# First layer's attention: the second half of each finished channel pair's split moved from step 25 to step 27 of its sixteen

## The chip, the core and the metric

The kernel runs on one core of one Trainium2 chip. The metric is the device time of one execution in microseconds; the figure shown for a kernel is the median of several executions. The profile is of one execution of its own.

The engines are called as the profile has them: PE is TensorE (matmul; PEld its weight load), DVE is VectorE, ACT is ScalarE, POOL is GpSimd, SP issues the DMAs.

## What is computed

Two layers over an input of 8 x 32 x 32 x 512, all in float32. Only the first is touched by the change. Cut to what matters, it is:

```python
x_norm = group_norm(x) * scale + bias                  # 32 groups of 16 channels
q, k, v = split(x_norm @ w_qkv + b_qkv)                # 8 heads of 64 channels, 1024 tokens, 8 images
weight = softmax((q * s) @ (k * s).T)                  # per image and head, 1024 x 1024
out = (weight @ v) @ w_out + b_out                     # (1)
x = x + out
```

The second layer is an attention with a depthwise convolution, sampled keys and values and an MLP. Products are made with operands in two parts, a rounded high part and the rest as a low part, so that three products of the parts stand for one in float32. "Split" below means making these two parts. For (1) the attention's result has to be split before it is multiplied with `w_out`.

## The kernel before

`layer0` goes through eight images. Per image there are the projections to q, k and v, then the attention over 8 heads, then the projection of the result with `w_out`, which runs together with the start of the next image. Each engine has its own program, written out by hand (`tensor_image`, `scalar_image`, `vector_image`, `gpsimd_image`, `sync_image`); semaphores tie them together. There is no scheduler: an engine does its instructions in the order of the code and waits where a count has not been reached.

**The attention's loop.** The 64 units of an image are 8 heads times 8 tiles of 128 query rows; the loop variable `i_` counts 64 steps and a few more at the end. In step `i_`, TensorE makes the scores of unit `i_` (lines L480 and L481, tile `a_ps`), transposes the exponentials of unit `i_`-2 (L495) and multiplies the transposed parts with v (L510). VectorE takes the row maximum of the scores (L647), ScalarE their exponential (L612, tile `a_prob`). The transposed tile is split: ScalarE writes the high part `ph` (L605, two per step) and VectorE the low part `pl` (L664, two per step). Two units make a block `b` of 256 queries of one head. On even steps ScalarE and VectorE add up the two halves of the block that was finished (L595 `a_fold_t`, L655 `a_fold_s`), VectorE takes reciprocals of row sums (L668), and GpSimd multiplies the block by them (L749), which writes the finished result over that head's q in the tile `qk`, all in SBUF.

**Staging.** A head needs its q and k in parts as well. SP copies them within SBUF (L397, L398, two heads ahead), and GpSimd makes the parts in the tiles `qs`, `kh` and `kl`: part 0 is a copy L725 and a two-input operation L727, part 1 the copies L731 and L734, part 2 the two-input operation L737. GpSimd takes a part before each of three consecutive blocks; for the heads staged while two heads of a pair run out, these stand between the L749 of the steps 24, 26, 28 and 30 (and again 16 steps later). L725 waits for the DMAs of the copies. L727 reads and writes SBUF only.

**The split in question.** Heads 2c and 2c+1 fill the 128 channels of pair `c`. When both are finished, `qk[:, c, :]` is split in two halves of 512 tokens: ScalarE copies to the high part `ah[c]` (L620) and VectorE subtracts it to the low part `al[c]` (L672), which reads two tiles of SBUF, `qk` and `ah`, and writes SBUF; the tiles show up as `a_a` in the profile. Both loops do this at the end of the steps in the table `SPLIT_AT`, which maps a step to a pair and a half. For the pairs 0 to 2 the steps are 23 and 25, 39 and 41, 55 and 57; the last pair goes in quarters after the loop. ScalarE waits for `att_ok`, the count of finished blocks (8 for pair 0), VectorE for ScalarE's part (`ah_ok`). The readers of the parts are the products with `w_out` in `out_tile`, which wait for six halves and come after step 64.

Of the kernel before, what the change touches and what calls it, by code (L numbers as in the profile page):

```python
# [24 lines left out]
CT = C // P  # L25
# [3 lines left out]
HALF = TOK // 2  # L29
# [53 lines left out]
def layer0(nc, x, gn_scale, gn_bias, w_qkv, b_qkv, w_out, b_out, x2, n_images=B):  # L83
# [7 lines left out]
    with ExitStack() as ctx:  # L91
# [90 lines left out]
        STAGE = 5  # L182
        AVERAGE_AT = 3
        POWER_AT = 3
        SPLIT_AT = {16 * c + 23 + 2 * s: (c, slice(s * HALF, (s + 1) * HALF)) for c in range(CT - 1) for s in range(2)}
        SPLIT_AT.update({U + 2 * j: (CT - 1, slice(256 * j, 256 * j + 256)) for j in range(NB)})
        SPLITS = 2 * (CT - 1)

# [188 lines left out]
        EACH.update({s.num: 16 * (U // 2 // ROWS) for s in iv_ld})  # L377
        EACH.update({staged.num: STAGE * NH, ah_ok.num: len(SPLIT_AT), al_ok.num: len(SPLIT_AT)})

# [184 lines left out]
        def scalar_image(act, r):  # L564
# [4 lines left out]
            def evict(g):  # L569

                kind, m, s = groups[g]
                act.wait_ge(pr_ps, at(pr_ps, g + 1))
                if r > 0 and g == 0:
                    act.wait_ge(al_ok, at(al_ok, 0))
                if r > 0 and g == 4:
                    act.wait_ge(o_st, at(o_st, 0))
                if kind == "v":
                    act.activation(v[:, :, m, 0:HD], by_head(ps[:, g % 8, :]), ACT.Copy).then_inc(vh_ok, 1)
                elif m < CT:
                    act.activation(qk[:, m, s * HALF:(s + 1) * HALF], ps[:, g % 8, :], ACT.Identity,  # L580
                                   bias=bq[:, m:m + 1], scale=QSCALE).then_inc(qk_sb, 1)
                else:
                    act.activation(qk[:, m, s * HALF:(s + 1) * HALF], ps[:, g % 8, :], ACT.Identity,
                                   bias=vec[:, 8 + m:9 + m]).then_inc(qk_sb, 1)
# [3 lines left out]
            for i_ in range(U + 7):  # L588
# [19 lines left out]
                if i_ < U:  # L608
# [6 lines left out]
                    if i_ < LATE:  # L615
                        evict(len(groups) - LATE + i_)
                if i_ in SPLIT_AT:
                    c, n = SPLIT_AT[i_]
                    act.wait_ge(att_ok, at(att_ok, 2 * NB * (c + 1) if c < CT - 1 else U // 2 - NB + (i_ - U) // 2 + 1))
# [9 lines left out]
        def vector_image(dve, r):  # L629
# [14 lines left out]
            for i_ in range(U + 7):  # L644
# [21 lines left out]
                if i_ >= 2 and i_ % 2 == 0 and i_ <= U:  # L666
                    dve.wait_ge(exp_ok, at(exp_ok, i_))
                    dve.reciprocal(row_inv[:, i_ - 2:i_], row_sum[:, i_ - 2:i_]).then_inc(inv_ok, 1)  # L668
                if i_ in SPLIT_AT:
                    c, n = SPLIT_AT[i_]  # L670
                    dve.wait_ge(ah_ok, at(ah_ok, list(SPLIT_AT).index(i_) + 1))
# [1275 lines left out]
def build(nc, a, out, n_images=B):  # L1947
    x2 = nc.dram_tensor("x2", [B, TOK, C], F32, kind="Internal").ap()
    l0 = [a["L0_conv_" + n] for n in ("gn_scale", "gn_bias", "w_qkv", "b_qkv", "w_out", "b_out")]
    layer0(nc, a["x"].rearrange("b h w c -> b (h w) c"), *l0, x2, n_images)  # L1950
    l1 = {n: a["L1_conv_" + n] for n in ("ln_g", "ln_b", "wq", "bq", "wv", "bv", "dw_w", "dw_b", "pw_w", "mq_w", "mq_b",
                                         "mk_w", "mk_b", "mv_w", "mv_b", "mo_w", "mo_b", "mlp_w", "mlp_b")}
    l1["dw_w"] = l1["dw_w"].rearrange("c o y x -> c (o y x)")
    l1["pw_w"] = l1["pw_w"].rearrange("k c y x -> k (c y x)")
    layer1(nc, x2, *l1.values(), out.rearrange("b h w c -> b (h w) c"), n_images)
# [17 lines left out]
```

## Time and profile before

| | us |
|---|---|
| median of 3 runs | 4020.2 |
| lowest, highest | 4017.14, 4028.37 |
| the profiled execution | 4022.35 |
| its span, first to last instruction | 4020.6 |

Mean granted TensorE clock over the span: 0.984. Of the span, the first 96.9 us go to the weights and the first image's start, and the eight attentions lie between 96.93 and 2272.32 us; the second layer takes about the last 1700. Between the attentions of two images there are some 98 us of projections.

A timeline row has the start, the duration, engine, line, operation and tiles as out<-in with their sizes; what stands in brackets is how long the engine sat idle before it and what ended that. Rows with x2 are two instructions in a row. Starts of neighbouring instructions on one engine can lie a little before the end of the one ahead. A windows row has the stretch, its length, the busy time of each engine, TensorE's granted clock as a share of 2.4 GHz, the DMA engines' share and GB/s.

### The profile page before, as it was taken

How to read it: one execution, taken by the hardware profiler on the slowest of the kernel's cores; microseconds unless marked ns; L12 is line 12 of the kernel's file. 1: busy time of each engine (PE TensorE's matmuls, PEld its weight loads, DVE VectorE, ACT ScalarE, POOL GpSimd, SP SyncE). 2: the span in 40 equal slices, each digit the busy share in tenths (PEclk: the TensorE clock that was granted, in tenths of full speed). 3: DMA queues.
4: the chain of work that ended last, by engine and by line, in shares of the span. 5: the costliest groups of instructions: out<-in, count | busy, mean ns of one | idle time of the engine just before them, and what ended most of it. 6: DMA issues, size and time to landing. Idle time of an engine off the chain costs nothing. (4 is left out here: it accounts for less than half of the span.)

```text
span 4020.6 us, 63404 instructions
## 1 busy us (share of the span) xinstructions
PE 3822.8 (95%) x21614; PEld 3202.9 (80%) x21614; DVE 2979.5 (74%) x5158; ACT 2433.8 (61%) x5241; POOL 1641.5 (41%) x1935
## 2 busy tenths in 40 slices
PE   8999999999999999999999889999999999999999
PEld 6888888888888888878888757777777777777777
DVE  3984984975966957939849747878787888787876
ACT  3873864755746837828738515656565656565656
POOL 1342432423432433324324305555545555555554
PEclk9999999999999999999999989999999999999999
DMA  2231331241241231322312222222222222222221
GB/s 87 53 75 44 65 75 43 53 89 41 54 90 36 54 80 41 62 67 54 77 47 59 74 96 69 74 74 74 74 74 74 75 75 73 75 73 75 73 74 59
DMA packets 175080, 269.32 MB, mean 67 GB/s; under 512 B 58732, under 2 KB 91560, under 8 KB 174760
## 3 DMA queue, kind: packets, MB, share of 16 engines
q1 hardware_dynamic: 170152, 248.48, 25.0%
q0 software_dynamic: 4608, 16.78, 1.4%
q8 instruction: 176, 2.88, 0.3%
q14 instruction: 144, 1.18, 0.2%
HBM read 113.90 MB, written 33.82 MB: 37 GB/s over the span
## 5 line engine op out<-in xcount | busy, mean ns | idle before, releaser
L647 DVE TENSOR_REDUCE a_neg_max<-a_ps 128x1 f32<-128x1024 f32 x512 | 622.3, 1217 | 313.9 <-PE a_ps L481 313.8
L605 ACT ACTIVATE a_ph<-a_ps 128x512 fp32r<-128x512 f32 x1024 | 565.8, 598 | 198.2 <-PE a_ps L495 196.8
L664 DVE TENSOR_TENSOR a_pl<-a_ps,a_ph 128x512 fp32r<-128x512 f32 x1024 | 655.4, 681 | 8.1 <-ACT a_ph L605 4.5
L749 POOL TENSOR_TENSOR a_qk<-a_fold_s,a_fold_r 64x256 f32<-64x256 f32 x256 | 192.5, 752 | 1060.9 <-DVE a_fold_s L655 840.5
L495 PE MATMUL a_ps<-a_ident,a_prob 128*128 128x128 f32 x4096 | 557.7, 278 | 56.7 <-DVE a_pl L664 55.6
L495 PEld LDWEIGHTS a_ps<-a_ident,a_prob 128*128 128x128 f32 x4096 | 464.3, 141 | 176.4 <-issue 113.6
L612 ACT ACTIVATE a_prob<-a_ps,a_neg_max 128x1024 f32<-128x1024 f32 x512 | 572.6, 1118 | 51.1 <-DVE a_neg_max L647 51.1
L510 PE MATMUL a_ps<-a_ph,a_v 128*128 128x256 f32 x2048 | 554.4, 303 | 0.0
L510 PE MATMUL a_ps<-a_pl,a_v 128*128 128x256 f32 x2048 | 513.2, 283 | 0.0
L481 PE MATMUL a_ps<-a_kl,a_qs 128*128 128x512 f32 x1024 | 406.4, 397 | 0.0
L480 PE MATMUL a_ps<-a_kh,a_qs 128*128 128x512 f32 x1024 | 404.7, 395 | 0.0
L1876 POOL TENSOR_SCALAR b_prob<-b_prob,b_row_inv 128x256 f32<-128x256 f32 x512 | 246.9, 482 | 366.7 <-DVE b_row_inv L1757 330.8
L510 PEld LDWEIGHTS a_ps<-a_pl,a_v 128*128 128x128 f32 x2048 | 392.5, 192 | 0.3
L510 PEld LDWEIGHTS a_ps<-a_ph,a_v 128*128 128x128 f32 x2048 | 389.0, 190 | 0.5 <-issue 0.2
L1651 DVE SCALAR_TENSOR_TENSOR b_ps<-b_qpad,b_dww,b_ps 128x256 f32<-128x256 f32 x704 | 294.2, 484 | 4.8
L1573 ACT ACTIVATE b_prob<-b_ps,b_neg_max 128x256 f32<-128x256 f32 x512 | 236.7, 483 | 42.8 <-DVE b_neg_max L1762 42.4
L1321 PE MATMUL b_ps<-b_qpad,b_diag 128*128 128x256 f32 x928 | 232.4, 409 | 0.0
L1321 PEld LDWEIGHTS b_ps<-b_qpad,b_diag 128*128 128x128 f32 x928 | 176.4, 190 | 50.9
L481 PEld LDWEIGHTS a_ps<-a_kl,a_qs 128*128 128x128 f32 x1024 | 195.2, 191 | 25.2
L725 POOL TENSOR_SCALAR a_kh<-a_qs 128x1024 fp32r<-128x1024 f32 x64 | 67.9, 1061 | 359.2 <-DMA a_kl<-a_qk 358.5
L480 PEld LDWEIGHTS a_ps<-a_kh,a_qs 128*128 128x128 f32 x1024 | 195.4, 191 | 22.2
L254 PE MATMUL a_ps<-a_xh,wqkv_hi 128*128 128x512 f32 x512 | 201.1, 393 | 5.6 <-DVE wqkv_lo L359 5.6
(262 smaller groups left out, 9218.7 us busy)
## 6 DMA issues: line engine op xcount, KB each, us to landing
a_qs<-a_qk SPq DMA_DIRECT2D x128, 256.0 KB, 4.3
a_kl<-a_qk SPq DMA_DIRECT2D x128, 256.0 KB, 4.8
a_xtok<-in_x SPq DMA_DIRECT2D x64, 256.0 KB, 5.4
a_fold_r<-a_inv_row SPq DMA_DIRECT2D x256, 64.0 KB, 3.6
b_xs<-x SPq DMA_DIRECT2D x64, 256.0 KB, 4.8
b_qs<-b_qh SPq DMA_DIRECT2D x64, 256.0 KB, 3.3
b_qs<-b_ql SPq DMA_DIRECT2D x64, 256.0 KB, 3.8
b_z<-x SPq DMA_DIRECT2D x64, 256.0 KB, 3.3
```

Source lines behind the costliest of these rows:

```text
L480: pe.matmul(bank, q_, kh[:, j, n], start=True, stop=False)
L481: mm = pe.matmul(bank, q_, kl[:, j, n], start=False, stop=True)
L495: mm = pe.transpose(ps[:, 4 + n % 2, kk * P:(kk + 1) * P], prob[:, u % 2, kt * P:(kt + 1) * P], ident[:])
L510: mm = pe.matmul(ps[:, 6 + b % 2, 0:256], v[:, h, kt, :], q_[:, b % 2, kt, :], start=kt == 0 and e == 0, stop=kt == TT - 1 and e == 1)
L605: act.activation(ph[:, b % 2, 4 * g:4 * g + 4, (u % 2) * P:(u % 2 + 1) * P], ps[:, 4 + n % 2, :].rearrange("p (k q) -> p k q", k=4), ACT.C ...
L612: act.activation(prob[:, i_ % 2, :], ps[:, 2 * (i_ % 2):2 * (i_ % 2) + 2, :] .rearrange("p a b -> p (a b)"), ACT.Exp, bias=neg_max[:, i_:i ...
L647: dve.tensor_reduce(neg_max[:, i_:i_ + 1], ps[:, 2 * (i_ % 2):2 * (i_ % 2) + 2, :] .rearrange("p a b -> p (a b)"), AX, ALU.max, negate=Tru ...
L664: dve.tensor_tensor(pl[here], ps[:, 4 + n % 2, :].rearrange("p (k q) -> p k q", k=4), raw(ph[here]), ALU.subtract).then_inc(pl_ok, 1)
L1321: mm = pe.matmul(ps[:, c, 0:NS], diag[:, e % DIAGS, :], window(c, n), start=first, stop=last)
L1573: act.activation(prob[:, u % 2, t, :], ps[:, 2 * (u % 2) + t // 2, (t % 2) * NK:(t % 2 + 1) * NK], ACT.Exp, bias=neg_max[:, c:c + 1], accu ...
L1651: dve.scalar_tensor_tensor(dst, window(c, n), dww[:, c, n:n + 1], grid(partial), ALU.mult, ALU.add).then_inc(tap, 1)
L1876: pool.tensor_scalar(prob[:, u % 2, t, :], prob[:, u % 2, t, :], row_inv[:, c:c + 1], 0.0, ALU.mult, ALU.add).then_inc(sc_ok, 1)
```

## The change

The second half of the pairs 0, 1 and 2 is split two steps later: at the steps 27, 43 and 59 instead of 25, 41 and 57. The first halves stay at 23, 39 and 55.

```diff
--- before.py
+++ after.py
@@ -182,7 +182,7 @@
         STAGE = 5
         AVERAGE_AT = 3
         POWER_AT = 3
-        SPLIT_AT = {16 * c + 23 + 2 * s: (c, slice(s * HALF, (s + 1) * HALF)) for c in range(CT - 1) for s in range(2)}
+        SPLIT_AT = {16 * c + 23 + 4 * s: (c, slice(s * HALF, (s + 1) * HALF)) for c in range(CT - 1) for s in range(2)}
         SPLIT_AT.update({U + 2 * j: (CT - 1, slice(256 * j, 256 * j + 256)) for j in range(NB)})
         SPLITS = 2 * (CT - 1)
```

On VectorE, steps 25 to 27 of the first image, before. `a_a_77` is the low part of pair 0, L647 begins a step:

```order
L647 TENSOR_REDUCE a_neg_max<-a_ps 128x1
L664 TENSOR_TENSOR a_pl<-a_ps,a_ph 128x4x128 x2
L672 TENSOR_TENSOR a_a_77<-a_qk,a_a_77 128x512
L647 TENSOR_REDUCE a_neg_max<-a_ps 128x1
L655 TENSOR_TENSOR a_fold_s<-a_ps,a_fold_t 64x256
L664 TENSOR_TENSOR a_pl<-a_ps,a_ph 128x4x128 x2
L668 RECIPROCAL a_row_inv<-a_row_sum 128x2
L647 TENSOR_REDUCE a_neg_max<-a_ps 128x1
L664 TENSOR_TENSOR a_pl<-a_ps,a_ph 128x4x128 x2
L647 TENSOR_REDUCE a_neg_max<-a_ps 128x1
```

and with the change:

```order
L647 TENSOR_REDUCE a_neg_max<-a_ps 128x1
L664 TENSOR_TENSOR a_pl<-a_ps,a_ph 128x4x128 x2
L647 TENSOR_REDUCE a_neg_max<-a_ps 128x1
L655 TENSOR_TENSOR a_fold_s<-a_ps,a_fold_t 64x256
L664 TENSOR_TENSOR a_pl<-a_ps,a_ph 128x4x128 x2
L668 RECIPROCAL a_row_inv<-a_row_sum 128x2
L647 TENSOR_REDUCE a_neg_max<-a_ps 128x1
L664 TENSOR_TENSOR a_pl<-a_ps,a_ph 128x4x128 x2
L672 TENSOR_TENSOR a_a_77<-a_qk,a_a_77 128x512
L647 TENSOR_REDUCE a_neg_max<-a_ps 128x1
```

L672 has moved behind the maximum L647, the fold L655, the splits L664 and the reciprocal L668 of two steps. It now stands between the last L664 of step 27 and the L647 of step 28.

On ScalarE, from the exponential of step 25 on, before (`a_a_77` is here the high part):

```order
L612 ACTIVATE a_prob,a_row_sum<-a_ps,a_neg_max 128x1024
L620 ACTIVATE a_a_77<-a_qk 128x512
L595 ACTIVATE a_fold_t<-a_ps 64x256
L605 ACTIVATE a_ph<-a_ps 128x4x128 x2
L612 ACTIVATE a_prob,a_row_sum<-a_ps,a_neg_max 128x1024
L605 ACTIVATE a_ph<-a_ps 128x4x128 x2
L612 ACTIVATE a_prob,a_row_sum<-a_ps,a_neg_max 128x1024
L595 ACTIVATE a_fold_t<-a_ps 64x256
```

and with the change:

```order
L612 ACTIVATE a_prob,a_row_sum<-a_ps,a_neg_max 128x1024
L595 ACTIVATE a_fold_t<-a_ps 64x256
L605 ACTIVATE a_ph<-a_ps 128x4x128 x2
L612 ACTIVATE a_prob,a_row_sum<-a_ps,a_neg_max 128x1024
L605 ACTIVATE a_ph<-a_ps 128x4x128 x2
L612 ACTIVATE a_prob,a_row_sum<-a_ps,a_neg_max 128x1024
L620 ACTIVATE a_a_77<-a_qk 128x512
L595 ACTIVATE a_fold_t<-a_ps 64x256
```

L620 has moved behind the exponentials of steps 26 and 27, and now stands right ahead of the fold copy L595 of step 28. The same happens for each pair and image. On TensorE, GpSimd and SP nothing stands in another place.

## Rows read from the trace of the kernel before

**Rows 1.** The page, section 1: busy us (share of the span), instructions
```profile
...
PE 3822.8 (95%) x21614; PEld 3202.9 (80%) x21614; DVE 2979.5 (74%) x5158; ACT 2433.8 (61%) x5241; POOL 1641.5 (41%) x1935
...
```

**Rows 2.** Windows of step 25 or 41 to 30 or 46: stretch and length, engines' busy us
```profile
...
734.07:751.83 17.76, 15.30 (x100) 13.87 (x99) 15.41 (x23) 12.58 (x24) 9.39 (x7) 0.90 0.10 21
...
1591.24:1606.44 15.20, 13.93 (x100) 12.38 (x99) 14.03 (x22) 12.51 (x24) 9.71 (x7) 1.00 0.21 44
...
1873.60:1888.08 14.48, 13.94 (x100) 12.39 (x99) 13.31 (x23) 12.52 (x24) 9.87 (x7) 1.00 0.21 47
...
2206.69:2223.04 16.35, 13.94 (x100) 12.39 (x99) 15.16 (x23) 12.53 (x24) 9.43 (x7) 1.00 0.10 22
sum 263.56, PE 233.47 PEld 208.29 DVE 235.18 ACT 200.51 POOL 152.64; mean PE 14.59 PEld 13.02 DVE 14.70 ACT 12.53 POOL 9.54
```

**Rows 3.** The same sixteen windows for line L672 alone: its busy time on VectorE
```profile
...
sum 263.56, DVE 32.41; mean DVE 2.03
```

**Rows 4.** Timeline of VectorE, third image, steps 25 to 28: start us, us, ...
```profile
...
737.07 2.60 DVE L672 TENSOR_TENSOR a_a<-a_qk,a_a 128x512 fp32r<-128x512 f32 x1 [0.61 <-ACT a_a L620]
739.60 1.21 DVE L647 TENSOR_REDUCE a_neg_max<-a_ps 128x1 f32<-128x1024 f32 x1
...
742.33 1.20 DVE L647 TENSOR_REDUCE a_neg_max<-a_ps 128x1 f32<-128x1024 f32 x1
...
746.32 1.23 DVE L647 TENSOR_REDUCE a_neg_max<-a_ps 128x1 f32<-128x1024 f32 x1 [1.14 <-PE a_ps L481]
```

**Rows 5.** Timeline of GpSimd, same image
```profile
...
736.74 2.38 POOL L727 TENSOR_TENSOR a_qs<-a_qs,a_kh 64x1024 fp32r<-64x1024 f32 x1
...
```

**Rows 6.** Timeline of TensorE, same image
```profile
...
741.88 1.94 PE L495 MATMUL a_ps<-a_ident,a_prob 128*128 128x128 f32 x8 [2.46 <-DVE a_pl L664]
...
```

**Rows 7.** Windows, same image: the column after POOL busy is TensorE's granted clock
```profile
...
743.00:745.00 2.00, 2.00 (x11) 2.00 (x10) 1.73 (x3) 1.74 (x3) 1.17 (x2) 0.50 0.21 37
...
```

**Rows 8.** Timeline of VectorE, seventh image, steps 23 to 29
```profile
...
1867.09 1.23 DVE L647 TENSOR_REDUCE a_neg_max<-a_ps 128x1 f32<-128x1024 f32 x1
...
1870.26 0.69 DVE L672 TENSOR_TENSOR a_a<-a_qk,a_a 128x512 fp32r<-128x512 f32 x1 [0.75 <-ACT a_a L620]
1870.87 1.22 DVE L647 TENSOR_REDUCE a_neg_max<-a_ps 128x1 f32<-128x1024 f32 x1
...
1873.60 1.20 DVE L647 TENSOR_REDUCE a_neg_max<-a_ps 128x1 f32<-128x1024 f32 x1
...
1876.60 0.69 DVE L672 TENSOR_TENSOR a_a<-a_qk,a_a 128x512 fp32r<-128x512 f32 x1 [0.61 <-ACT a_a L620]
1877.21 1.22 DVE L647 TENSOR_REDUCE a_neg_max<-a_ps 128x1 f32<-128x1024 f32 x1
...
1879.94 1.20 DVE L647 TENSOR_REDUCE a_neg_max<-a_ps 128x1 f32<-128x1024 f32 x1
...
1882.57 1.22 DVE L647 TENSOR_REDUCE a_neg_max<-a_ps 128x1 f32<-128x1024 f32 x1 [0.23 <-PE a_ps L481]
...
1885.33 1.23 DVE L647 TENSOR_REDUCE a_neg_max<-a_ps 128x1 f32<-128x1024 f32 x1
...
```

**Rows 9.** Timeline of GpSimd, seventh image
```profile
...
1878.29 2.37 POOL L727 TENSOR_TENSOR a_qs<-a_qs,a_kh 64x1024 fp32r<-64x1024 f32 x1
...
1882.69 1.05 POOL L734 TENSOR_SCALAR a_kh<-a_kl 128x1024 fp32r<-128x1024 f32 x1
...
```

**Rows 10.** Timelines of GpSimd and of VectorE, sixth image, step 25
```profile
...
1594.08 1.05 POOL L725 TENSOR_SCALAR a_kh<-a_qs 128x1024 fp32r<-128x1024 f32 x1 [3.16 <-DMA a_kl<-a_qk]
1595.21 2.69 POOL L727 TENSOR_TENSOR a_qs<-a_qs,a_kh 64x1024 fp32r<-64x1024 f32 x1
...
1594.24 1.42 DVE L672 TENSOR_TENSOR a_a<-a_qk,a_a 128x512 fp32r<-128x512 f32 x1 [0.61 <-ACT a_a L620]
...
```

**Rows 11.** Windows between the attentions of two images, columns as in rows 2
```profile
...
280.85:379.33 98.48, 95.11 (x461) 78.92 (x460) 37.74 (x64) 29.76 (x49) 30.03 (x22) 1.00 0.25 72
...
1702.15:1802.26 100.11, 96.73 (x461) 80.05 (x460) 37.28 (x64) 29.74 (x49) 30.28 (x23) 0.98 0.25 72
...
```

## The prediction

> **What bounds the kernel now.** I read four views in this order: the page's busy shares, the windows by stage, the timelines of single engines around steps 23 to 30, and the clock column of the windows.
>
> TensorE is 95% busy over the span [rows 1], but a mean over stages says nothing of this stretch. In the attention of layer one each step runs in a ring: TensorE makes scores, VectorE takes their maximum (L647), ScalarE the exponential (L612), TensorE transposes, ScalarE and VectorE split the transposed tile in two (L605, L664), TensorE uses it. A step is measured from one L647 to the next. Undisturbed it lasts 2.63 or 2.76 us [rows 8], so whatever stops VectorE for longer than the ring's slack stops TensorE too.
>
> The place to look at is the stretch from step 25 to step 30, which occurs 16 times with the next head's staging beside it (eight images, channel pairs 0 and 1). Its length should be the same each time, since its instructions are. It is not: the shortest is 14.48 us, others take 15.20, 16.35 or 17.76 us, and all sixteen take 263.56 us [rows 2]. Sixteen times 14.48 is 231.68, so **31.88 us** are lost there. Seven of the sixteen are like the 17.76, three like the 16.35, four are longer than 14.48 by up to 0.8, as the 15.20 is, and two stand at 14.48.
>
> The same windows for VectorE's split L672 alone show who loses it: 32.41 us for sixteen instructions [rows 3], where an undisturbed one takes 0.69 us [rows 8], that is 21.37 us too much. In the third image the split starts at 737.07 us and takes 2.60 [rows 4]; GpSimd's L727, a two-input operation of 2.38 us on SBUF, started at 736.74 and ends at 739.12 [rows 5]. The other nine long ones look alike: the split of step 25 lies on an L727 already running and waits for its end.
>
> The rest, 31.88 - 21.37 = 10.51 us, is TensorE's clock. After the held split TensorE stood idle for 2.46 us [rows 6], and just then its granted clock reads 0.50, which is 1.2 GHz instead of 2.4 [rows 7]; step 27 to 28 then lasts 746.32 - 742.33 = 3.99 us [rows 4] instead of 2.63 [rows 8]. Only the seven longest stretches show a clock below 1.00 (0.90 on average); 10.51 / 7 is 1.50 us each.
>
> **What the change does.** Per image and pair one ScalarE copy L620 and one VectorE split L672 move from the end of step 25 to the end of step 27. Nothing is added. The orders of TensorE, GpSimd and the SP queue, its DMAs among them, are the same; no queue is passed but VectorE's and ScalarE's own. Behind the moved pair on their engines stand the fold and the splits of step 28. Its wait for finished blocks (att_ok 8) was met before step 25 and stays met. Its output is wanted by the final projection only, steps later, so a later split costs no reader anything; even for pair 2, at step 59, the projection is several steps away.
>
> *Term one, the collision at step 25: -31.9 us.* With no split there, L727 meets only VectorE's L647, L655, L664 and L668: in the seventh image it ran beside them from 1878.29 to 1880.66, and step 26 still took 1879.94 - 1877.21 = 2.73 us [rows 8, 9]. All of the 21.37 us goes, and with it the TensorE pause and the 10.51 us at the low clock.
>
> *Term two, the split at step 27: does it meet GpSimd again?* What follows L727 there is the product L749 of a finished block, then two copies of the staging, L731 and L734, then a long idle until step 28's fold. In the undisturbed seventh image L727 starts at 1878.29 and L734 ends at 1882.69 + 1.05 = 1883.74, 5.45 us later [rows 9]. The split moves by how much? At step 25 it starts 1876.60 - 1873.60 = 3.00 us after L647; a split after an ordinary step, as step 23's is, starts 1870.26 - 1867.09 = 3.17 us after [rows 8]. Step 27 will be of that kind, and start 2.63 + 2.76 = 5.39 us after step 25's L647 (two steps of the kind that now follow, 1879.94 to 1882.57 to 1885.33 [rows 8]). So it moves by 5.39 + 3.17 - 3.00 = 5.56 us. In the ten long cases L727 starts about 0.33 us before the old split [rows 4, 5], so L734 ends 5.45 - 0.33 = 5.12 us after the old split's place, and the new split comes 0.44 us later than that. Clear, though not by much.
>
> In the late cases, where the DMA that releases L725 landed late, nothing is gained by the shift. In the sixth image L725 ends at 1594.08 + 1.05 = 1595.13, 0.89 us into the old split of 1594.24, which took 1.42 [rows 10], 0.73 more than 0.69: a split pays the overlap less 0.16. Afterwards L727 starts 0.08 behind, L734 ends at 1595.21 + 5.45 = 1600.66, and the new split wants to start at 1594.24 + 5.56 = 1599.80; overlap 0.86, price 0.70. So the four medium cases meet L734 for what they met L725 for. Their total is 21.37 less ten times 1.91 (2.60 - 0.69 [rows 4, 8]), 2.3 us. I add back **+2.3 us**. Pauses of that size were followed by no low clock (15.20 us at clock 1.00 [rows 2]).
>
> The Trainium skill bears on this term (SBUF — State Buffer, "Who interferes with whom"): a VectorE operation with two SBUF inputs and a GpSimd operation that reads SBUF exclude each other for a whole instruction, whichever shape they have. The trace agrees [rows 4, 5, 10], copies included. The rule speaks against the new place, for it makes L731 and L734 as able to block as L727; only their length is smaller. It gives no time by itself; the one it would give is that of the first rival below.
>
> *Term three, the ring's own cost of a split: +1.2 us.* Two splits two steps apart cost steps of 3.78, 2.73, 3.61, 2.73, 2.63, 2.76, 2.75 (step 23 to 30, 1867.09 to 1888.08: 20.99 us [rows 2, 8]). Four apart I expect 3.78, 2.73, 2.63, 2.76, 3.78, 2.73, 2.63 = 21.04, each number one of the same rows. That is +0.05, 24 times (pair 2 too). Bounds: 0, if the pair of steps costs the same, and +0.17 each (3.78 - 3.61), 4.1 us.
>
> **Sum**, against the profiled execution's 4022.35 us: 4022.35 - 31.9 + 2.3 + 1.2 = **3994 us**. The median of the three runs is 2 us lower; how often they collided isn't seen, and after the change the time depends little on that, so I keep 3994, 26 us (0.65%) under the median. A measurement can tell about 0.3% (12 us) from no change.
>
> **Rivals.**
> First, the copies take L727's place. The 0.44 us of clearance hangs on 5.39 us for two steps and on 3.17. Were the split a little over half a microsecond earlier, or GpSimd later, all would meet L734 [rows 9]. The price is at most its 1.05 less 0.16, 0.9 us, in the twelve places now free of it: +10.7, **4005 us**. For it: the thin margin. Against: in undisturbed stretches the steps repeat closely, as 2.73 us before and after the split of step 25 does [rows 8].
>
> Second, the slower clock appears elsewhere. Between two attentions a stretch takes 98.48 us, or 100.11 with clock 0.98 [rows 11], in two of seven cases; a later or earlier arrival of everything may make that none or seven: -3.3 to +8.1, **3991 to 4002 us**. The second layer has dips too, so some microseconds more may shift.
>
> Third, no gain: the collision only marks a place where the ring would wait anyway, for a later transfer or for scores. Then **4022 us**. Against: in the 14.48 us cases nothing waits [rows 2].
>
> Fourth, slower: L727 itself still runs when the new split comes. It must then start 5.56 + 0.33 - 2.38 = 3.5 us later than in the long cases (2.67 us into step 25, 3.00 - 0.33), so past 6.2 us into that step. The latest of the sixteen is the seventh image's, at 1878.29, 4.69 us into it [rows 8, 9]. The price is 1.91, with the low clock 3.41 us a place; in all sixteen 54.6, **4046 us**; with 30.7 us to be eaten up it turns the sign from ten places on. SP's order is unchanged, so nothing in the profile pushes it there.
>
> **How the numbers follow.** Forecast 0.78, first rival 0.11, second 0.05, third 0.04, fourth 0.02. The first two rivals are still faster than the bound of 4008. Faster by over 0.3%: 0.93, within: 0.05, slower: 0.02. The range: downwards the medium cases and the clock between attentions may vanish (2.3 + 3.3) and the second layer vary by a few, 3985; upwards the first rival and term three's upper bound, 4006.
>
> **What would show it.** Right: L672 long nowhere (no 2.6 us; a few between 0.7 and 1.5), the stretches from step 25 to 30 alike within 1 us, most at about 14.5 us, clock 1.00 in all of them, step 25 to 26 at 2.63 and step 27 to 28 at 3.78. First rival: L672 at 1 to 1.6 us in most of sixteen, behind L734. Wrong altogether: L672 at 2.6 us still, or L672 short and the stretches still 16 us or longer with another releaser in VectorE's idle time.

## The result, and the profile after

| | before | after |
|---|---|---|
| median, us | 4018.67 (4 runs) | 3994.9 (4 runs) |
| lowest, highest | 4016.38, 4028.37 | 3989.44, 4001.9 |
| the profiled execution | 4022.35 | 4001.9 |
| its span | 4020.6 | 4000.0 |

The ratio is 0.9936, 95% interval 0.9918 to 0.9954: faster by 0.64%. Ratios, here and below, are taken over all executions and differ a little from the quotient of the two medians. The forecast was 3994 us. A second measurement, beside other kernels, gave 0.9924 (0.9907 to 0.9940).

The page of the changed kernel, the line that answers to [rows 1]. TensorE's busy time is the same to 1 us, VectorE's is 21 us less:

```profile
...
PE 3823.4 (96%) x21614; PEld 3202.0 (80%) x21614; DVE 2958.2 (74%) x5158; ACT 2430.6 (61%) x5241; POOL 1640.5 (41%) x1935
...
```

The sixteen stretches of five steps from 25 or 41, answering to [rows 2], with columns as there:

```profile
...
211.79:226.99 15.20, 13.93 (x100) 12.38 (x99) 13.97 (x23) 12.56 (x24) 9.42 (x7) 1.00 0.21 40
447.65:462.19 14.54, 13.95 (x100) 12.39 (x99) 13.30 (x23) 12.57 (x24) 9.43 (x7) 1.00 0.10 21
...
1335.69:1350.81 15.12, 13.94 (x100) 12.39 (x99) 13.89 (x23) 12.57 (x24) 9.41 (x7) 1.00 0.18 40
...
sum 233.86, PE 223.07 PEld 198.22 DVE 214.12 ACT 201.04 POOL 150.97; mean PE 13.94 PEld 12.39 DVE 13.38 ACT 12.57 POOL 9.44
```

They came down from 263.56 to 233.86 us. Fourteen of them lie between 14.53 and 14.59 us, two at 15.12 and 15.20, and the clock is 1.00 in all. The same windows for L672 alone, answering to [rows 3] (it lies inside them, in step 27 or 43):

```profile
...
211.79:226.99 15.20, 1.36 (x1) 1.00 0.21 40
447.65:462.19 14.54, 0.69 (x1) 1.00 0.10 21
...
sum 233.86, DVE 12.39; mean DVE 0.77
```

12.39 us instead of 32.41. Sixteen undisturbed ones would be 11.09 (0.69 each), so of the 21.3 us for which the splits were held, 1.3 are left.

VectorE in the first image from step 25 on. L647 begins a step, and this answers to [rows 4, 8]:

```profile
...
165.45 1.20 DVE L647 TENSOR_REDUCE a_neg_max<-a_ps 128x1 f32<-128x1024 f32 x1
...
168.09 1.23 DVE L647 TENSOR_REDUCE a_neg_max<-a_ps 128x1 f32<-128x1024 f32 x1 [0.24 <-PE a_ps L481]
...
170.84 1.23 DVE L647 TENSOR_REDUCE a_neg_max<-a_ps 128x1 f32<-128x1024 f32 x1
...
174.01 0.69 DVE L672 TENSOR_TENSOR a_a<-a_qk,a_a 128x512 fp32r<-128x512 f32 x1 [0.75 <-ACT a_a L620]
174.62 1.22 DVE L647 TENSOR_REDUCE a_neg_max<-a_ps 128x1 f32<-128x1024 f32 x1
...
177.35 1.20 DVE L647 TENSOR_REDUCE a_neg_max<-a_ps 128x1 f32<-128x1024 f32 x1
...
179.99 1.23 DVE L647 TENSOR_REDUCE a_neg_max<-a_ps 128x1 f32<-128x1024 f32 x1 [0.24 <-PE a_ps L481]
```

Steps of 2.64, 2.75, 3.78, 2.73 and 2.64 us; the split starts 8.56 us after step 25 does. GpSimd beside it, answering to [rows 5, 9]:

```profile
...
168.17 2.39 POOL L727 TENSOR_TENSOR a_qs<-a_qs,a_kh 64x1024 fp32r<-64x1024 f32 x1
170.64 0.73 POOL L749 TENSOR_TENSOR a_qk<-a_fold_s,a_fold_r 64x256 f32<-64x256 f32 x1
171.46 1.05 POOL L731 TENSOR_SCALAR a_qs<-a_kh 64x1024 fp32r<-64x1024 f32 x1
172.60 1.05 POOL L734 TENSOR_SCALAR a_kh<-a_kl 128x1024 fp32r<-128x1024 f32 x1
176.30 0.73 POOL L749 TENSOR_TENSOR a_qk<-a_fold_s,a_fold_r 64x256 f32<-64x256 f32 x1 [2.65 <-DVE a_fold_s L655]
...
```

L734 ends at 172.60 + 1.05 = 173.65, the split comes at 174.01: 0.36 us apart. TensorE's longest pause in the steps 27 to 30 is now 0.59 us, where 2.46 stood [rows 6]:

```profile
...
176.91 1.17 PE L495 MATMUL a_ps<-a_ident,a_prob 128*128 128x128 f32 x8 [0.59 <-DVE a_pl L664]
...
```

The eight attentions, from the first L647 of an image to its last, before and then after, in the sum line of the windows by stage:

```profile
...
sum 1482.83, PE 1430.66 PEld 1263.17 DVE 1343.03 ACT 1220.80 POOL 555.54; mean PE 178.83 PEld 157.90 DVE 167.88 ACT 152.60 POOL 69.44
```

```profile
...
sum 1453.67, PE 1420.43 PEld 1253.18 DVE 1321.68 ACT 1219.45 POOL 553.39; mean PE 177.55 PEld 156.65 DVE 165.21 ACT 152.43 POOL 69.17
```

They gave 29.2 us. The whole span fell by only 20.6 in these two executions, because the second layer, which the change does not touch, took 11.5 us more in the second one (the start took 2.8 less). Its windows, before and after:

```profile
...
2272.32:4020.60 1748.28, 1646.26 (x8179) 1323.80 (x8177) 1344.05 (x2678) 973.36 (x2578) 856.48 (x1288) 0.98 0.26 76
...
```

```profile
...
2240.20:4000.00 1759.80, 1658.79 (x8179) 1335.06 (x8177) 1344.06 (x2678) 971.74 (x2578) 857.63 (x1288) 0.97 0.26 75
...
```

VectorE's, ScalarE's and GpSimd's work there is the same within 2 us; TensorE's clock is 0.97 instead of 0.98. TensorE's busy time over the span is the same for that reason: 10.2 us less in the attentions, 12.5 more in the second layer. A second profiled execution of the changed kernel, 6.4 us shorter, has 1453.40 us of attentions and 6.1 us less of second layer. So an effect of this size is better read from the stage that was changed than from one profiled span.

### The profile page after: what moved, and what is told of

Its sections match the earlier page's. It is cut to its first block and busy times, and to the rows that moved or that the text cites. A ratio compares the mean times of both kernels' runs of the same rounds, so it can differ in the third digit from the quotient of the medians.

```text
span 4000.0 us, 63404 instructions
## 1 busy us (share of the span) xinstructions
PE 3823.4 (96%) x21614; PEld 3202.0 (80%) x21614; DVE 2958.2 (74%) x5158; ACT 2430.6 (61%) x5241; POOL 1640.5 (41%) x1935
## 3 DMA queue, kind: packets, MB, share of 16 engines
q14 instruction: 144, 1.18, 0.2%
## 5 line engine op out<-in xcount | busy, mean ns | idle before, releaser
L647 DVE TENSOR_REDUCE a_neg_max<-a_ps 128x1 f32<-128x1024 f32 x512 | 621.9, 1216 | 303.8 <-PE a_ps L481 303.8
L664 DVE TENSOR_TENSOR a_pl<-a_ps,a_ph 128x512 fp32r<-128x512 f32 x1024 | 654.1, 679 | 7.0 <-ACT a_ph L605 3.7
L749 POOL TENSOR_TENSOR a_qk<-a_fold_s,a_fold_r 64x256 f32<-64x256 f32 x256 | 191.7, 749 | 1039.0 <-DVE a_fold_s L655 864.4
L725 POOL TENSOR_SCALAR a_kh<-a_qs 128x1024 fp32r<-128x1024 f32 x64 | 67.4, 1053 | 352.7 <-DMA a_kl<-a_qk 352.0
```

Of the source, the lines that this page charges most:

```text
L647: dve.tensor_reduce(neg_max[:, i_:i_ + 1], ps[:, 2 * (i_ % 2):2 * (i_ % 2) + 2, :] .rearrange("p a b -> p (a b)"), AX, ALU.max, negate=Tru ...
L664: dve.tensor_tensor(pl[here], ps[:, 4 + n % 2, :].rearrange("p (k q) -> p k q", k=4), raw(ph[here]), ALU.subtract).then_inc(pl_ok, 1)
```

## The experiments

Two theories. The **port theory** is that of the prediction: VectorE's L672, which reads two SBUF tiles, and GpSimd's L727, which reads SBUF, exclude each other; the long ones of these pauses bring TensorE's low clock with them. The name is a label: what the runs can show is that the two don't run at the same time. The **spacing theory** is its rival: GpSimd is a bystander, and two splits within three steps leave a backlog in the ring that four steps of distance let drain. All runs were timed against the kernel before on the same chip; I compare ratios.

### Pair 2 alone

```diff
-        SPLIT_AT = {16 * c + 23 + 2 * s: ...
+        SPLIT_AT = {16 * c + 23 + (4 if c == 2 else 2) * s: ...
```

> The kernel before, with the second half moved from step 57 to 59 for pair 2 alone; pairs 0 and 1 keep 25 and 41. Pair 2 has no staging beside it. Port theory (VectorE's L672 is held by GpSimd's L727, and the TensorE pause that follows brings the low clock): nothing gained, +0.05 us in each of eight images, so the time of before within 0.1%, and in steps 25 to 30 and 41 to 46 the same mixture of 14.5, 15.2, 16.4 and 17.8 us. Spacing theory (two splits two steps apart leave a backlog in the ring, four apart do not): a third of the gain of 24 us, about 8 us or 0.2% faster.

Measured: 4026.78 us against 4023.34, ratio 1.0004 (0.9992 to 1.0015). The upper end of what the interval leaves for a gain is 0.08%, the spacing theory's third of the gain was 0.2%. The sixteen stretches of pairs 0 and 1 look as they did before:

```profile
...
497.36:511.83 14.47, 13.93 (x100) 12.39 (x99) 13.29 (x21) 12.50 (x24) 9.40 (x7) 1.00 0.10 25
...
1636.70:1653.12 16.42, 13.93 (x100) 12.38 (x99) 15.25 (x21) 12.50 (x24) 9.42 (x7) 1.00 0.10 22
...
2157.55:2175.49 17.94, 15.46 (x100) 14.01 (x99) 15.43 (x22) 12.58 (x24) 9.41 (x7) 0.90 0.09 21
...
sum 268.49, PE 236.44 PEld 211.25 DVE 237.39 ACT 200.50 POOL 151.62; mean PE 14.78 PEld 13.20 DVE 14.84 ACT 12.53 POOL 9.48
```

So where nothing of the staging runs beside it, moving the split is worth nothing. The port theory stands, the spacing theory fails its first test. The trace of the kernel before had said so already: the eight stretches of pair 2 (steps 57 to 62), with the two splits two steps apart as everywhere, all last 14.48 or 14.49 us. GpSimd has two instructions in them, where the sixteen have seven:

```profile
...
833.31:847.79 14.48, 13.93 (x100) 12.38 (x99) 13.30 (x22) 12.51 (x24) 1.48 (x2) 1.00 0.37 52
...
```

### Steps 28, 44 and 60

```diff
-        SPLIT_AT = {16 * c + 23 + 2 * s: ...
+        SPLIT_AT = {16 * c + 23 + 5 * s: ...
```

> Second halves at the steps 28, 44 and 60, one step later than in the changed kernel, five steps from the first half. Port theory: the split now starts about 3.2 us into step 28 and meets GpSimd's L737 (2.39 us, from 2.50 to 4.89 us into that step, released by the fold and not by a DMA, so in all sixteen places): L672 takes 0.69 + 4.89 - 3.17 - 0.16 = 2.25 us, 25 us more than the changed kernel in sum, and up to 24 us more where the low clock follows: 4019 to 4043 us. Spacing theory: as fast as the changed kernel or faster, 3994 us.

Measured: 4020.8 us against 4023.34, ratio 0.9996 (0.9983 to 1.0010). One step further than the change, and its gain is gone. VectorE and then GpSimd, first image, step 28:

```profile
...
173.27 1.22 DVE L647 TENSOR_REDUCE a_neg_max<-a_ps 128x1 f32<-128x1024 f32 x1 [0.34 <-PE a_ps L481]
...
176.43 2.28 DVE L672 TENSOR_TENSOR a_a<-a_qk,a_a 128x512 fp32r<-128x512 f32 x1 [0.35 <-ACT a_a L620]
178.64 1.21 DVE L647 TENSOR_REDUCE a_neg_max<-a_ps 128x1 f32<-128x1024 f32 x1
...
```

```profile
...
174.95 0.75 POOL L749 TENSOR_TENSOR a_qk<-a_fold_s,a_fold_r 64x256 f32<-64x256 f32 x1 [1.67 <-DVE a_fold_s L655]
175.78 2.38 POOL L737 TENSOR_TENSOR a_kl<-a_kl,a_kh 128x1024 fp32r<-128x1024 f32 x1
```

The split wants to start at 176.43, 3.16 us into its step, L737 has been running since 175.78 and ends at 178.16; the split takes 2.28 us, 2.25 were expected. It is so in all sixteen places, 26 us over 0.69 in sum:

```profile
...
165.13:180.97 15.84, 2.28 (x1) 1.00 0.13 24
...
781.89:798.06 16.17, 2.62 (x1) 1.00 0.12 24
...
sum 254.04, DVE 37.09; mean DVE 2.32
```

The attentions together last 1478.16 us, 24.5 more than with the split at 27. The low clock followed in fewer places than feared: five low-clock spells begin inside attentions, at some 1.4 us each (an attention of 185.19 us has one, one of 183.80 none). That alone doesn't make the 24.5: 26.0 less 1.3, plus five times 1.4, is 31.7. The rest comes back in the step behind: with the split at step 28, step 29 lasts 2.33 us (178.64 to 180.97), where step 28 behind a split at 27 lasts 2.73. From step 23 to 30 that leaves 0.3 us less per pair, the hold set aside, and 7 us in 24; it was not foreseen. One of the five spells, of the fifth image, in the windows view (clock 0.62); it follows one of two splits that were held for 1.9 us and not 1.6:

```profile
...
1317.00:1321.50 4.50, 4.50 (x24) 3.89 (x22) 3.50 (x7) 2.77 (x7) 0.74 (x1) 0.62 0.02 0
...
```

### L727 cut to half

```diff
-                    pool.tensor_tensor(qs[HD:P, j, :], raw(qs[HD:P, j, :]), raw(hi[HD:P, :]), ALU.subtract)\
+                    pool.tensor_tensor(qs[HD:P, j, 0:HALF], raw(qs[HD:P, j, 0:HALF]), raw(hi[HD:P, 0:HALF]), ALU.subtract)\
```

> The kernel before (splits at 23 and 25), with GpSimd's L727 cut to half of its columns, so it leaves out the low part of q for the second 512 tokens. Port theory: L727 lasts 1.2 instead of 2.39 us, so a long L672 takes 0.69 + 1.2 - 0.33 - 0.16 = 1.4 us instead of 2.6; ten times 0.7 and 2.3 us for the late cases remain of the 21.4, and the pauses are too short for the low clock, so its 10.5 us go too: about 22 us faster than before, 3997 us. Spacing theory: no change, 4019 us, since GpSimd's work is on nobody's way.

Measured: 4006.91 us against 4023.34, ratio 0.9954 (0.9938 to 0.9970). Splits at 23 and 25 as before, and no instruction of VectorE, ScalarE or TensorE changed. The kernel leaves out the low part of q for the second 512 tokens, and serves for its time alone. GpSimd in the third image, and the split beside it:

```profile
...
732.25 1.28 POOL L727 TENSOR_TENSOR a_qs<-a_qs,a_kh 64x512 fp32r<-64x512 f32 x1
...
```

```profile
...
732.59 1.49 DVE L672 TENSOR_TENSOR a_a<-a_qk,a_a 128x512 fp32r<-128x512 f32 x1 [0.61 <-ACT a_a L620]
...
```

L727 takes 1.28 us, ends at 733.53, 0.94 us into the split, which takes 1.49 us: 0.80 too long, the overlap less 0.14. In the stretches:

```profile
...
729.59:744.86 15.27, 13.93 (x100) 12.39 (x99) 14.10 (x23) 12.51 (x24) 8.29 (x7) 1.00 0.12 25
...
1294.12:1308.59 14.47, 13.93 (x100) 12.39 (x99) 13.29 (x21) 12.51 (x24) 8.82 (x7) 1.00 0.11 25
...
sum 242.33, PE 222.99 PEld 198.23 DVE 223.46 ACT 200.11 POOL 134.79; mean PE 13.94 PEld 12.39 DVE 13.97 ACT 12.51 POOL 8.42
```

```profile
...
sum 242.33, DVE 21.77; mean DVE 1.36
```

Over 231.68 us, sixteen times 14.48, the stretches lose 10.65; over 11.09 the splits lose 10.68. The whole loss is the time that the splits are held, and nothing is left for the clock, which is 1.00 in all sixteen. I had expected 9.3: L727 lasts 1.28 us at half size and not 1.2, and eleven of the sixteen places met it in this execution where I had counted ten (two more met L725). The attentions are 21.2 us shorter than before (1461.65), where about 22 were expected. The total gained about 18 by the ratio (0.46% of 4020) instead of 22; the interval, 12 to 25, holds both.

### Staging one block later

```diff
-                if 1 <= k <= NH - 2 and part < 3:
-                    stage(k + 1, (part,))
+                if 1 <= k <= NH - 2 and part in (1, 2):
+                    stage(k + 1, ((0,), (1, 2))[part - 1])
```

> The kernel before, splits untouched at 23 and 25; instead GpSimd takes part 0 of the staging (L725, L727) one block later, behind the product L749 of step 26, and parts 1 and 2 together behind that of step 28. Port theory: L725 starts about 1.8 us into step 26, 2.8 us after the split of step 25 has ended, so L672 takes 0.69 us in all sixteen places, every stretch from step 25 to 30 lasts 14.5 us with clock 1.00, and the whole 31.9 us go: 3987 us, a little below the changed kernel. Spacing theory: no change. A third possibility, that the staging then comes too late for the scores of step 32 or 48: TensorE would wait there, at most some 2 us a time, and the time would lie above 3987 by up to 30 us.

Measured: 3989.35 us against 4023.34, ratio 0.9915 (0.9898 to 0.9932). The splits are where they were, and the whole gain is there. Every stretch is 14.47 or 14.48 us:

```profile
...
166.63:181.10 14.47, 13.94 (x100) 12.39 (x99) 13.29 (x21) 12.50 (x24) 7.74 (x7) 1.00 0.12 25
212.89:227.37 14.48, 13.95 (x100) 12.40 (x99) 13.29 (x23) 12.51 (x24) 7.74 (x7) 1.00 0.20 42
...
sum 231.58, PE 223.00 PEld 198.26 DVE 212.71 ACT 200.06 POOL 123.56; mean PE 13.94 PEld 12.39 DVE 13.29 ACT 12.50 POOL 7.72
```

```profile
...
sum 231.58, DVE 11.08; mean DVE 0.69
```

The attentions last 1450.88 us, 32.0 less than before, where 31.9 were worked out. The third possibility, a staging too late for the scores of step 32, did not come true. This is the clearest answer to the spacing theory: no split moved, all the loss gone.

### The change once more, and step 29

The first kernel is the change itself. The second:

```diff
-        SPLIT_AT = {16 * c + 23 + 2 * s: ...
+        SPLIT_AT = {16 * c + 23 + 6 * s: ...
```

> The changed kernel once more, beside the others of this call: 3994 us or 0.64% under before. In its trace L672 of step 27 and 43 takes 0.69 us except where the DMA before L725 landed late (up to 1.4 us), its stretches from step 25 to 30 last 14.5 us, and no low clock falls inside an attention. What differs between executions is the number of low-clock spells in the second layer.

> Second halves at the steps 29, 45 and 61. Port theory: L737 runs from about 2.5 to 4.9 us after the start of step 28, which ends before the split of step 29 wants to start (2.73 + 3.17 = 5.9 us after the start of step 28), and L734 is long over even in the late cases: L672 takes 0.69 us everywhere, about 1 to 2 us less in sum than the changed kernel, which no timing resolves: 3993 us. With the 16 long L672 of step 28 gone, this and the kernel with the splits at step 28 differ by one step and by some 25 us. Spacing theory: the same time for 27, 28 and 29.

Measured against 4020.66 us: the change 3992.93, ratio 0.9924 (0.9907 to 0.9940); step 29 3996.41, ratio 0.9935 (0.9918 to 0.9953). They can't be told apart. In step 29's trace each L672 of the second half takes 0.69 us, late DMA or not (windows of steps 26 to 31):

```profile
...
sum 240.37, DVE 11.09; mean DVE 0.69
```

The attentions last 1455.44 us, though, against 1453.40 for the change measured beside it. What was won on late cases (1.1 us) was more than lost on the ring: at step 29 I expected the same price of a split, and it is higher, by 3.1 us in 24. Steps 27, 28, 29 thus give a gain, none, and a gain, as GpSimd's work runs, and not as the distance grows.

### ScalarE's copy a step ahead

This starts from the kernel with the staging one block later. While reading these timelines another cost stood out: VectorE idles 0.75 or 0.61 us before each split, waiting for ScalarE's copy that is made in the same step [rows 8]. So the copies get a table of their own, one step earlier:

```diff
+        COPY_AT = {i_ - (i_ < U): e for i_, e in SPLIT_AT.items()}
...
-                if i_ in SPLIT_AT:
-                    c, n = SPLIT_AT[i_]
+                if i_ in COPY_AT:
+                    c, n = COPY_AT[i_]
                     act.wait_ge(...
```

with the splits at 23 and 25, and in the second kernel at 22 and 24 (`16 * c + 22 + 2 * s`).

> The kernel with GpSimd's staging one block later and VectorE's splits at 23 and 25, and ScalarE's copies L620 now one step ahead of them, at 22 and 24. With both on the same step VectorE idles 0.75 and 0.61 us for the copy and then takes 0.69. If that idle time is what a split costs the ring, 48 times 0.7 = 33 us go, less what the copy costs ScalarE in the step before (0.63 us, where ScalarE idles 0.2 to 0.6 a step): 3960 to 3985 us, and the steps 23 and 25 fall from 3.78 and 3.61 to about 3.1. If the two costs only part company, nothing is gained: 3989 us.

> The same with both one step earlier: ScalarE's copies at 21 and 23, where ScalarE has no fold copy in that step, VectorE's splits at 22 and 24. VectorE has the fold and the reciprocal there, 0.55 us more than on odd steps. GpSimd's L749 ends about 2.4 us into steps 22 and 24, ahead of the split at 2.8, so no collision: L672 takes 0.69. Same sum as the other, 3960 to 3985 us; whichever of the two puts its work where the engine has more idle time is the faster one, by a few microseconds.

Measured against 4020.66 us: 3956.76, ratio 0.9836 (0.9816 to 0.9855), and 3962.15, ratio 0.9847 (0.9828 to 0.9865). Both beat the change and the kernel before. VectorE in the first image of the first one (its L648 and L673 are the other kernels' L647 and L672):

```profile
...
156.85 1.23 DVE L648 TENSOR_REDUCE a_neg_max<-a_ps 128x1 f32<-128x1024 f32 x1 [0.24 <-PE a_ps L482]
...
159.60 1.22 DVE L648 TENSOR_REDUCE a_neg_max<-a_ps 128x1 f32<-128x1024 f32 x1
...
161.94 0.68 DVE L673 TENSOR_TENSOR a_a<-a_qk,a_a 128x512 fp32r<-128x512 f32 x1
162.54 1.22 DVE L648 TENSOR_REDUCE a_neg_max<-a_ps 128x1 f32<-128x1024 f32 x1
...
165.27 1.20 DVE L648 TENSOR_REDUCE a_neg_max<-a_ps 128x1 f32<-128x1024 f32 x1
...
167.59 0.68 DVE L673 TENSOR_TENSOR a_a<-a_qk,a_a 128x512 fp32r<-128x512 f32 x1
168.19 1.21 DVE L648 TENSOR_REDUCE a_neg_max<-a_ps 128x1 f32<-128x1024 f32 x1
...
```

The idle time before the split is gone, and steps 23 and 25 last 2.94 and 2.92 us instead of 3.78 and 3.61; ScalarE's copy fits into its own idle time of the step before, which stays at 2.75. The attentions last 1414.37 us, 36.5 less than with the staging alone. With the copies on odd and the splits on even steps they last 1423.29, 9 us more; The expectation that no split would meet GpSimd there was wrong: three of the 48 were held, two by its product L749 and one by the staging's L737, and took 1.09, 1.18 and 1.11 us. That explains 1.4 of the 9. VectorE has the fold and the reciprocal in those steps, which may be why the rest is there, though no run took that apart.

## Why the prediction was right

**What bounds the stretch.** Right. The reading that the stretches of five steps ought to be equal and that 31.88 us are lost in them is confirmed from two sides: the change brought them from 263.56 to 233.86, and the later staging to 231.58, sixteen times 14.47.

**Term one, -31.9 us.** Right in both parts. No L672 at 2.6 us is left, and with them went the low clock: no clock below 1.00 in any of the sixteen. That the low clock hung on the long pause, and did not come by itself, is shown by the half L727: pauses kept but shortened, clock whole. In no profiled execution without a split held for 1.6 us or more does a low-clock spell begin inside an attention (seven executions); in the three with such splits there are seven, nine and five.

**Term two, +2.3 us.** The mechanism was right, the size was 1.3. The split came 8.56 us after step 25's start, 5.39 + 3.17 by the prediction, and L734 ended 0.36 to 0.47 us before it in the nine ordinary places like the one shown (0.44 forecast). Late landings of the DMA met L734 as worked out: at 220.35 a split took 1.36 us, 0.67 too long. In this execution two cost something (15.20 and 15.12 us) and one a trace of it (14.59); at one very late landing the split came between L731 and L734 and cost nothing (14.54), a case that the sum had not got. Which landings are late differs from one execution to the next, and no run shows why.

**Term three, +1.2 us.** Right: 1453.67 less the 1.3 of term two, against 1482.83 less 31.9, is 1.4. The step lengths came one by one as listed, 2.64, 2.75, 3.78, 2.73, 2.64.

**The sum.** -28.4 us for the attentions, -29.2 measured. The 3994 of the forecast and the median of 3994.9 agree better than they deserve to: the unchanged second layer varies by more than ten microseconds from one execution to another, which the range covered in part by its 'some microseconds'.

**The rivals.** First: did not come; the clearance was as thin as said, yet fourteen of the sixteen splits lost at most 0.06 us. Eleven were clear of GpSimd, by 0.18 us or more. Second: the low clock between attentions came twice again, and in the second layer more often, +11.5 us in the profiled execution. It was the largest thing that the sum had not got. Between the attentions the profiled executions had from none to five such spells in seven places, and no run shows what decides it. Third, no gain: refuted. Fourth: its place was wrong but its kind is real; one step further on, at 28, GpSimd's L737 does to the split what L727 did at 25, and the gain is lost.

**The rule.** The Trainium skill (SBUF — State Buffer, "Who interferes with whom") has it that the two exclude each other for a whole instruction and that the order of issue decides. The runs agree where L725, L727, L734 and L737 were running when the split came: each time it ended 0.5 to 0.6 us after GpSimd's instruction. It works the other way round too: where the split came first, an L727 that started 0.45 us before the split's end took 2.69 us instead of 2.38 [rows 10]. VectorE's L647, L655 and L664, with at most one operand in SBUF, ran beside L727 at their usual length (L647 at 1.23 us), as the Trainium skill has it in the same section.

## What to carry to other kernels

In a loop whose passes ought to be equal, compare the length of the same stretch in every pass: the shortest is what it can do, and the difference summed is what a repair can give. For an instruction of VectorE with two SBUF operands, write down where GpSimd's instructions lie in the same step, with their ends, before choosing its place; moving either of the two is enough, and a place released by the ring itself is safer than one that hangs on a DMA's landing. When a stall goes away, look at the idle time in front of what was stalled: here taking that away gave as much again.

## What was not expected

The low clock after a pause is not a matter of the pause alone. Before, seven of ten splits held for some 1.9 us were followed by it, and nine of eleven in the run with pair 2 alone. With the split at step 28, four of fourteen held for 1.6 us were, and one of two held for 1.9. With the half L727, held for 0.5 to 1.0 us, none of thirteen. So pauses of one size fall on either side, and the longer ones more often on the low one.

A held split does not pay the whole overlap. It started before GpSimd's instruction had ended by 0.89, 0.94 or 2.05 us and took 0.73, 0.80 or 1.91 longer than 0.69: 0.14 to 0.16 us of the overlap are not paid; what the split does in them no run shows. In the changed kernel a split at 220.35 overlapped L734, which ran from 220.11 for 1.06 us, by 0.82 us and took 0.67 longer.

The copy on ScalarE was nearly free one step earlier. The estimate was a step of 3.1 us and the trace shows 2.94, so the 33 us that looked like an upper bound became 36.5 in the attentions.
